# A gated cross-attention block on one NeuronCore: new prologue, new instruction order, and four of twelve value-weight remainders on GpSimd

## What is computed

```python
x = x + tanh(g_xattn) * xattn(layernorm(x), ctx, mask, rms_scale, q_w, kv_w, out_w)
x = x + tanh(g_ffn)   * ffn(layernorm(x), W1, b1, W2, b2)

# xattn: xn, mn = rmsnorm(x), rmsnorm(ctx); q = rope(xn @ q_w) / 8; k = rope(mn @ k_w); v = mn @ v_w
#        probs = softmax(where(mask, q @ k.T, -2.38e38)); out = sum over heads of (probs @ v) @ out_w[h]
# ffn:   h = gelu(x @ ternary(W1).T + b1); out = h @ ternary(W2).T + b2
# ternary(w): scale = mean(|w|); clip(round(w / scale), -1, 1)
```

## Time and profile before

| | |
|---|---|
| median of 3 runs | 316.05 us |
| the profiled execution: its own time | 316.32 us |
| its span, first to last instruction | 314.5 us |
| TensorE, VectorE, ScalarE, GpSimd busy | 95%, 80%, 74%, 41% |
| `fill()` ends (TensorE's first product of step 2) | 86.4 us |
| granted TensorE clock in the profile | 1.00 throughout |

### The profile page before, as it was taken

The page is one execution under the profiler, slowest core; times in us unless marked ns, Lnnn a source line. Parts: engine busy times, 40 slices in busy tenths (PEclk is TensorE's granted clock), DMA queues, the critical chain, the costliest instruction groups (busy, mean ns, idle before and its releaser), DMA issues.

```text
span 314.5 us, 6809 instructions
## 1 busy us (share of the span) xinstructions
PE 299.4 (95%) x2143; PEld 277.2 (88%) x2143; DVE 252.8 (80%) x823; ACT 233.9 (74%) x601; POOL 127.7 (41%) x149
## 2 busy tenths in 40 slices
PE   4998799978999999999999999999999999999996
PEld 4987679876899899998999899989998899889886
DVE  2599999998998699868898789779986898567443
ACT  1457785888869894989587977888589959784581
POOL 7241687876043332363146205432334313611300
PEclk9999999999999999999999999999999999999999
DMA  7980000020021002010011002100201000200101
GB/s 216 231 269 1 1 2 0 6 65 0 3 67 53 17 2 67 4 67 2 19 48 50 17 0 67 50 17 0 70 33 37 0 2 1 69 0 1 69 0 67
DMA packets 12281, 13.27 MB, mean 42 GB/s; under 512 B 823, under 2 KB 11696, under 8 KB 12256
## 3 DMA queue, kind: packets, MB, share of 16 engines
q1 hardware_dynamic: 11452, 12.29, 12.2%
q0 software_dynamic: 96, 0.21, 0.6%
q10 hardware_dynamic: 708, 0.46, 0.5%
HBM read 8.76 MB, written 4.19 MB: 41 GB/s over the span
## 4 chain that ended last, share of the span: by engine, by line
PE 83%; DVE 10%; issue 2%; ACT 2%; DMA 1%; POOL 0%; ACTq 0%; DVEq 0%
PE ps_m L1262 22%; PE ps_h L1262 20%; PE ps_m L1487 17%; PE ps_s L1262 8%; PE ps_t L1270 4%; PE ps_t L1435 4%; PE ps_t L1411 2%; PE ps_t L1507 1%; PE ps_m L1507 1%; PE ps_h L1276 1%; PE ps_t L1443 1%; DVE s_neg L999 1%; DMA gate_row<-in_gates 1%; DVE vw_lo L890 1%; ACT hT_hi L658 1%
## 5 line engine op out<-in xcount | busy, mean ns | idle before, releaser
L457 POOL TENSOR_TENSOR prob<-prob,p_inv 128x512 f32<-128x512 f32 x32 | 33.8, 1055 | 63.9 <-DVE p_inv L1008 63.9
L1053 DVE TENSOR_TENSOR hT_lo<-h_all,hT_hi 128x512 fp32r<-128x512 f32 x64 | 42.2, 686 | 18.4 <-ACT hT_hi L658 18.3
L1262 PE MATMUL ps_h<-x1nT_hi,w_tern 128*128 128x512 f32 x128 | 54.3, 425 | 2.3 <-ACT hT_hi L658 2.1
L1487 PE MATMUL ps_m<-w_tern,hT_hi 128*128 128x256 f32 x224 | 55.3, 287 | 0.0
L624 ACT ACTIVATE prob<-s_neg,s_min 128x154 f32<-128x154 f32 x128 | 52.5, 415 | 1.8 <-DVE s_min L1003 1.8
L1487 PE MATMUL ps_m<-w_tern,hT_lo 128*128 128x256 f32 x224 | 53.6, 279 | 0.0
L433 POOL TENSOR_TENSOR q_cos<-q_cos,q_sin 128x256 f32<-128x256 f32 x32 | 23.6, 736 | 69.0 <-DVE q_sin L966 68.2
L1262 PE MATMUL ps_h<-x1nT_lo,w_tern 128*128 128x512 f32 x128 | 50.5, 395 | 0.0
L658 ACT ACTIVATE h_all<-ps_h,b_sb 128x512 f32<-128x512 f32 x64 | 44.3, 692 | 8.1 <-PE ps_h L1262 6.9
L1262 PE MATMUL ps_m<-vw_hi,pT_hi 128*128 128x256 f32 (+1 forms) x160 | 45.5, 284 | 0.0
L1262 PE MATMUL ps_m<-vw_hi,pT_lo 128*128 128x256 f32 (+1 forms) x160 | 44.8, 280 | 0.0
(11 more groups left out here) (160 smaller groups left out, 789.7 us busy)
## 6 DMA issues: line engine op xcount, KB each, us to landing
x_sb<-in_x SPq DMA_DIRECT2D x8, 512.0 KB, 3.5
out_x<-x_both SPq DMA_DIRECT2D x8, 384.0 KB, 2.5
h_all<-in_w1t SPq DMA_DIRECT2D x1, 1024.0 KB, 11.0
w_raw<-in_w2t SPq DMA_DIRECT2D x1, 1024.0 KB, 13.4
out_x<-x_both SPq DMA_DIRECT2D x8, 128.0 KB, 1.7
x_both<-in_ctx_main SPq DMA_DIRECT2D x1, 512.0 KB
wo_raw<-in_wo SPq DMA_DIRECT2D x2, 256.0 KB, 8.6
x_both<-in_wq ACTq DMA_DIRECT2D x1, 256.0 KB, 6.4
```

The lines of the kernel that those rows point to most:

```text
L457: pool.tensor_tensor(main, main, inv.to_broadcast([P, H, P]), ALU.mult)
L1053: dve.tensor_tensor(hT_lo[:, c, :], h_act[c % 4][:], hT_hi[:, c, :], ALU.subtract).then_inc(h_split, 1)
L1262: m = pe.matmul(dst, lhs, rhs, start=(n == 0), stop=(n == len(pairs) - 1))
L1487: m = pe.matmul(dst, a[:, c, P * t:P * (t + 1)], w[:, c, :], start=(c == 0 and a is hT_hi), stop=(c == NF - 1 and a is hT_lo))
```

## The change

- **Scales.** The paired row is no longer copied: four small products pick the scale row's elements with strides and write half columns (`spread_pairs`), and two more plus the gates' one follow (`spread_rows`). The second `keep_warm(5)` is left out, as are later ones (11 of 25 products stay). The keys' scales no longer wait for the other ones.
- **Moved to GpSimd.** The addition of the rotated keys (one instruction of 128x640 in place of two of 128x320), the mask biases, `b2_gated`, and the remainders of pieces 3, 4, 6 and 7 (`VW_ON_POOL`). For these ScalarE writes a second, unrounded copy of the bank into `vw_wide` (two buffers in `x1n`, idle then), from which GpSimd subtracts. The bank comes free with the high part.
- **Row minima.** In the unrolled steps `mask_and_min` uses the combined add-and-minimum for all four heads (four instructions in place of five); the loop keeps the old form.
- **Order.** All four `fill()` lists are rewritten, with `FILL_T`, `FILL_M` and `FILL_H`.

```diff
+        vw_wide = [x1n[:].rearrange("p t d -> p (t d)")[:, GT * j:GT * (j + 1)] for j in range(2)]
...
-        FILL_H = (0, 1, 2, "total", 3, 4, 5, 6, 7, 8, 9, 10, 11)
+        FILL_H = (0, "total", 1, 2, 3, 4, 5, 6, 7, 8, 9, 10, 11)
+        VW_ON_POOL = (3, 4, 6, 7)
...
+            def add_rotated_keys():
+                pool.wait_ge(k_products_done, 4)
+                a, b = (k[:].rearrange("p t (o j) c -> p t o (j c)", o=1).to_broadcast([P, CT, 2, C])
+                        for k in (k_a, k_b))
+                pool.tensor_tensor(k_rot, a, b, ALU.add).then_inc(k_rotated, 1)
...
+            def vw_rest(n):
+
+                k = VW_ON_POOL.index(n)
+                pool.wait_ge(vw_hi_set, n + 1)
+                hi, cols = vw_slot(vw_hi, *VW[n])
+                pool.tensor_tensor(vw_slot(vw_lo, *VW[n])[0], vw_wide[k % 2][:, cols], hi,
+                                   ALU.subtract).then_inc(vw_pool_set, 1)
...
                 act.wait_ge(vw_filled, n + 1)
                 dst, cols = vw_slot(vw_hi, *VW[n])
+                if n in VW_ON_POOL:
+                    k = VW_ON_POOL.index(n)
+                    if k >= 2:
+                        act.wait_ge(vw_pool_set, k - 1)
+                    nc.scalar.activation(vw_wide[k % 2][:, cols], h_bank(n)[:, cols], ACT.Copy, scale=vw_gate(*VW[n]))
                 nc.scalar.activation(dst, h_bank(n)[:, cols], ACT.Copy, scale=vw_gate(*VW[n])).then_inc(vw_hi_set, 1)
...
-            def pair_scale_row():
-                dve.wait_ge(rows_in, 32)
...
+            def pair_scales():
+                dve.wait_ge(pairs_spread, 1)
+                dve.tensor_scalar(scale1[:, 0:KD], ps_m[0][:, 0:KD], 1.0, None, ALU.add).then_inc(pair_scale_set, 1)
...
-                dve.wait_ge(k_products_done, 4)
-                for j in range(2):
-                    dve.tensor_tensor(k_rot[:, :, j, :], k_a[:].rearrange("p t j c -> p t (j c)"),
-                                      k_b[:].rearrange("p t j c -> p t (j c)"), ALU.add).then_inc(k_rotated, 1)
...
+                if isinstance(s.i, int):
+                    for h in range(H):
+                        m = dve.tensor_tensor_reduce(
+                            sn[:, h, :], ps_s[h // 2][:, S * (h % 2):S * (h % 2 + 1)], mask_now[:],
+                            1.0, 3.4e38, ALU.add, ALU.min, least[:, h:h + 1])
+                    m.then_inc(s_masked, 1)
+                    return
...
                     before = FILL_H[n - 2]
                     if before == "total":
                         pe.wait_ge(w_scaled, 1)
+                    elif before in VW_ON_POOL:
+                        pe.wait_ge(vw_hi_set, before + 1)
                     else:
-                        pe.wait_ge(vw_set, before + 1)
+                        pe.wait_ge(vw_set, before + 1 - vw_pooled(before))
...
                 keep_warm(5)
-                spread_scales()
-                keep_warm(5)
+                spread_pairs()
+                spread_rows()
                 context_tail_T()
```

More of the change, by code:

```diff
@@ L316, in flamingo_block, with vw_pooled @@
         V_PARTS = ((slice(0, B * P), ps_m[1][:]), (slice(B * P, CT * P), ps_h[0][:, KD * P:KD * P + P]))
+        def vw_pooled(n):
+            return sum(m < n for m in VW_ON_POOL)
         def vw_gate(b, h):
@@ L874, in kk_rest @@
                         dve.tensor_tensor(dst, src, hi, ALU.subtract).then_inc(kk_set, 1)
-            def mask_biases():
-                dve.wait_ge(mask_in, 16)
-                dve.tensor_scalar(mask_bias[:], mask_u8[:], MASK_FILL, -MASK_FILL, ALU.mult,
-                                  ALU.add).then_inc(mask_f_set, 1)
-            def gate_b2():
-                dve.wait_ge(gate_set, 1)
-                dve.wait_ge(b2_in, 16)
-                dve.tensor_scalar(b2_gated[:], b2_raw, gate[:, 1:2], None, ALU.mult).then_inc(b2_set, 1)
             def vw_rest(n):
+                assert n not in VW_ON_POOL
                 dve.wait_ge(vw_hi_set, n + 1)
@@ L1144, in fill @@
                 tail_lo(SECOND, 0)
-                q_lo(SECOND, 3)
                 sums2_there(SECOND)
                 statistics2(SECOND)
-                ternary(2)
+                ternary(4)
+                p_lo(SECOND, 0)
+                shift2(SECOND)
                 vw_rest(9)
-                inverse(SECOND, 2)
-                shift2(SECOND)
-                ternary(3)
                 mask_and_min(SECOND, 3)
-                ternary(4)
-                tail_lo(SECOND, 1)
                 p_lo(SECOND, 1)
                 vw_rest(10)
-                residual(SECOND, 0)
+                tail_lo(SECOND, 1)
+                ternary(5)
+                inverse(SECOND, 2)
+                sums1(SECOND)
                 x1n_lo(SECOND, 0)
@@ L1276, in keep_warm, with spread_pairs, spread_rows @@
                     pe.matmul(dst[:, 0:P], ones_sb[:], ones_sb[:], start=True, stop=True)
-            def spread_scales():
+            def spread_pairs():
                 pe.wait_ge(const_set, 2)
                 pe.wait_ge(rows_in, 32)
-                pe.wait_ge(rows_paired, 1)
                 for k in range(KD):
-                    pe.matmul(ps_m[1][:, 2 * k:2 * k + 2],
-                              scale_pairs[:, k].rearrange("o h q -> o (h q)"), ones_sb[0:1, 0:2],
-                              start=True, stop=True)
+                    for half in range(2):
+                        rows = scale_row.rearrange("o (q k h) -> o k h q", k=KD, h=2)[:, k, half]
+                        m = pe.matmul(ps_m[0][C * half:C * (half + 1), k:k + 1], rows, ones_sb[0:1, 0:1],
+                                      start=True, stop=True)
+                m.then_inc(pairs_spread, 1)
+            def spread_rows():
                 for k in range(KD):
-                    pe.matmul(ps_m[1][:, 2 * KD + 2 * k:2 * KD + 2 * k + 2],
-                              scale_row.rearrange("o (p k) -> o k p", k=KD)[:, k], ones_sb[0:1, 0:2],
-                              start=True, stop=True)
-                pe.matmul(ps_m[1][:, 8:10], ones_sb[0:1, :], gate_row[:], start=True, stop=True).then_inc(rows_spread, 1)
+                    pe.matmul(ps_m[1][:, k:k + 1], scale_row.rearrange("o (p k) -> o k p", k=KD)[:, k],
+                              ones_sb[0:1, 0:1], start=True, stop=True)
+                pe.matmul(ps_m[1][:, KD:KD + 2], ones_sb[0:1, :], gate_row[:],
+                          start=True, stop=True).then_inc(rows_spread, 1)
             def context_T(k):
```

293 lines of the change are left out of this document (152 added, 141 removed), and 6 rows, old and new, of the table FILL_T.

## The result

| | before | after |
|---|---|---|
| median | 316.02 us | 312.92 us (4 runs, 312.73 to 313.64) |
| profiled execution: own time | 316.32 us | 312.73 us |
| its span | 314.5 us | 310.9 us |

The ratio is 0.9909, with a 95% interval of 0.9891 to 0.9927: the change is faster, and the medians are 3.1 us apart. The prediction had the sign, but its 309.1 us (6.9 us faster) are 3.8 us too low, and its range, which ended at 312.7, misses the time by 0.2 us.

A forecast was written before the change was run, and what follows sets the result against it. VectorE's queue was taken to set the prologue, the first 86.4 us, with TensorE bounding the rest. Gains 3.9 + 3.4 - 0.5 + 0.1 = 6.9 us gave 309.1 us; range 306.0 to 312.7.

The forecast's parts named there:

- the first rival: GpSimd becomes the bound, its full queue delaying the second norm's inverse root: 311.9 us, up to 312.7; chance 0.19.
- Piece 1: Start of the kernel up to the keys' remainders: they end at 24.1 instead of 28.04 us, 3.9 us gained.
- high parts 1.5 us, two rotations beside them: Between keys' transposes and remainders: high parts take 1.5 us with rotations alongside, then remainders 1.7 us, ending at 24.1.
- may go or return: 0 here: Waits for the port VectorE shares with GpSimd: counted as 0, with 0.8 us either way in the range.
- The 3.0 us that the removed addition was credited with: Ahead of the keys' remainders: two key-addition instructions leave VectorE's queue, taking 3.0 us out of it.
- Piece 2: From the keys' remainders to the end of step two's normalised input: VectorE's queue shrinks from 43.25 to 39.85 us.
- The gaps cannot shrink for nothing; I charge 0.5 us: Same stretch up to 71.30 us: four engines above 90% hand work to each other, so new gaps cost 0.5 us.
- The second rival: The start gives less, through a late context or TensorE staying slow up to 17.1 us: 311.5 us; chance 0.10.
- Four remainders leave it, -2.64: VectorE's queue before 71.30 us: four 128x512 remainders at 0.66 us each move away, -2.64 us.
- The minima: VectorE's queue before 71.30 us: one instruction fewer in each of eight `mask_and_min`, 0.22 us each, -1.76 us.
- the ledger: Sum of VectorE's instruction savings and additions before 71.30 us: -2.64, -1.76, -0.3 and +1.3, together -3.4 us.
- Piece 3: Gelus and last attention: ScalarE's 13.26 us chain stays; eight fewer VectorE instructions in steps 6 and 7 give 0 to 0.2 us.

The follow-up runs named there:

- k_keys: Changed kernel with `gate_norms` moved earlier and 17 warming products put back, plus the key addition returned from GpSimd to VectorE: 310.78 us.
- b_warm: Changed kernel with 17 idle-time warming products put back on TensorE between 21.8 and 31.6 us: 313.18 us, stretch 45.97 us.
- q_warm: Changed kernel with the warming products put back, run once more on another chip: 312.14 us, stretch 45.97 us.
- e_cnone: Changed kernel with `gate_norms` moved earlier and warming products put back, plus all twelve value-weight remainders on VectorE, without second copies: 312.95 us.
- f_ctwo: Changed kernel with `gate_norms` moved earlier and warming products put back, but only remainders 3 and 6 on GpSimd, 4 and 7 on VectorE: 311.76 us.
- a_gate: Changed kernel with one VectorE instruction, `gate_norms`, moved ahead of the second input remainder, before GpSimd's long `wo_rest`: 312.42 us.

## Why the prediction was wrong

**Right.** The bound, the place of the gain and the parts that stay: 227.6 us from ScalarE's first high part of step 2's queries (86.86 and 83.30 us) to the end in both kernels, the gelu stretch 13.27 us. Context transposes at 7.68 (7.8), keys' transposes at 19.67 (19.6), key addition hidden with 2.7 us to spare. That GpSimd would be full and hold the inverse root was the first rival, and the signs named for it (no gaps, VectorE waiting for an inverse root) are what came, from 43 us on. Its price was not: 2.8 us, of which a slow mask conversion was to be 1.9, against 0.8 measured and a conversion of 0.71 us.

**Piece 1, the step that failed: "high parts 1.5 us, two rotations beside them".** It took the keys' remainders to 24.1 us; they ended at 25.67, a head start of 2.4 in place of 3.9 us. The transposes came as forecast (19.67 against 19.6), so the error lies behind them. From their start to that of the remainders the forecast leaves 2.8 us, near the kernel before (2.89); the terms written out there, 1.5 and 1.7, reach only to 22.8, and the 1.3 us left for the rotations were not worked out. It took 4.25 us. Of the missing 1.45 us, 0.97 are the collision. The prediction noted that waits for the port "may go or return: 0 here", and looked only at instructions with two SBUF inputs; the one that was caught has one tensor input and four columns, right where `wo_rest` now runs. The remaining 0.5 us stays when the collision is gone (KT 3.28). The trace has the rotations for it: the first projection now stands behind the keys' transposes, and VectorE waits 1.1 us for it ahead of the rotations. No run moved it. The 3.0 us that the removed addition was credited with were not one gain but two causes; the instruction was worth nothing at its new place (k_keys), the collision stayed.

**Piece 2, two terms.** Forecast -3.4 + 0.5 = -2.9 us, measured -1.2 (48.19 to 47.00). *"The gaps cannot shrink for nothing; I charge 0.5 us"*: the change leaves out `keep_warm` products, and no term had the clock in this stretch. The second rival put it before 17 us. It came at 32 us and cost 1.0 us (b_warm, q_warm), 1.6 in the second execution of the changed kernel. *"Four remainders leave it, -2.64"*: they brought 1.2 us (e_cnone), since GpSimd's queue was full: its subtraction takes 1.29 to 1.58 us, not 1.04, and two of the four moves brought nothing (f_ctwo). Taking GpSimd's share away gives 0.8 us back. The minima were 1.3 in place of 1.76 us. With the clock and GpSimd out of the way the stretch is 45.10, 3.1 us under before and near the ledger's 3.4. That is in part luck: its two large terms gave 3.3 us of 4.4 (minima 1.3, remainders 2.0), and the terms counted against the change, +1.0 with `b2_gated`, cost only 0.2 (e_cnone is 1.1 us under before where the minima alone are 1.3). Of the 1.7 us that the stretch missed, the clock is 1.1, the remainders 1.4 and the minima 0.5; these small terms and the charge for gaps were 1.3 too high.

The sum, in profiled times: 6.9 - 1.5 (head) - 1.7 (stretch) - 0.1 = 3.6 us.

**Piece 3: 0 to 0.2 us forecast, none measured.** It passed over 1.3 us that neither kernel used, the table load, with its own row in the trace of before:

```profile
71.70 1.09 ACT L603 ACTIVATE xT_hi<-ps_t 128x512 fp32r<-128x512 f32 x2 [1.25 <-PE ps_t L1270]
...
73.18 1.28 ACT L658 ACT_TABLE_LOAD   x1 [0.40 <-PE ps_h L1262]
```

**The rule cited against the change** (the Trainium skill, Perfetto Trace Analysis, "Optimizing Scalar/DVE Operations": GpSimd and VectorE share a read port, so a shift between them may not help) would have given 311.7 us, nearer to the measured 312.9 than the sum, as the GpSimd rival's 311.9 was. The four remainders brought 1.2 of 2.64 us, and not nothing. The runs show GpSimd's queue as one reason and do not separate the port from it; the collision that is shown by itself hit an instruction that was never moved. A more exact rule was to be had: the Trainium skill, SBUF — State Buffer, "Who interferes with whom", says that a `tensor_scalar` can run in a mode that takes both ports, and then waits for GpSimd's whole instruction or holds it up. The trace agrees: `gate_norms` is one (1.88 us beside `wo_rest`), and so is L950 (0.79 us beside GpSimd at 58.70 us, 0.17 in the median). A rotation (L993), which reads PSUM and one SBUF input, took 0.48 us beside `wo_rest` in a_gate and 0.48 with GpSimd idle in the changed kernel.

**The range** treated causes as rivals that exclude each other. Here a part of one (GpSimd, 0.8), a form of another (the clock, 1.0) and the collision (1.0) came together, and each alone would have been inside. The ends given for the forecast do not follow from the terms named for them either: 0.8 and 0.5 below 309.1 are 307.8, 0.8 and 1.0 above it 310.9, where 307.5 and 310.7 stand.

## What to carry to other kernels

When an instruction that collides with another engine's is removed, ask which one will now stand beside the long partner: the wait belongs to the pair in time, not to the instruction, and moving the small victim ahead of it is the cheap remedy. Work taken from a full engine is worth only what the receiving engine has free in the same stretch, so two are to be weighed against each other, and half the move may bring all of the gain. When warming products are left out, read the granted clock of the stretch behind them as well. And where an engine is idle ahead of a stretch that starts with a table load, a dummy activation may pay; here it was worth 1.3 us in both kernels.
